# Gated cross-attention blocks on one Trainium2 core: GpSimd adds key blocks' exponentials, one TensorE product fewer in each sum, new order in the second half of a turn

## The chip, the cores and the metric

The kernel runs on one core of a Trainium2 chip. The metric is the device time in microseconds (us) of one execution. TensorE multiplies matrices, VectorE and ScalarE work element by element and read TensorE's results from PSUM, GpSimd works on SBUF, and SyncE (SP) issues the transfers.

## The reference

Two gated blocks, each an attention and a feed-forward part, over 8 batches of 256 rows and 512 features. The change touches only the second block's attention:

```python
q = rms_norm(linear(x, q_w, q_b), norm_q_w).reshape(B, L, NH, HD)      # 16 heads of 32
k_img = rms_norm(linear(ctx_img, k_img_w, k_img_b), norm_k_img_w)...   # 256 keys
v_img = linear(ctx_img, v_img_w, v_img_b)...
def attention(q, k, v):
    scores = jnp.einsum('bqhd,bkhd->bhqk', q, k) * scale
    probs = jax.nn.softmax(scores, axis=-1)
    return jnp.einsum('bhqk,bkhd->bqhd', probs, v)
x = x + tanh(g_xattn[1]) * (attention(q, k_img, v_img) @ o_w + o_b)    # then the quantised feed-forward part
```

## The kernel before, in words

The work has stages: a (first attention), b (first feed-forward part), and a last stage in which c (second attention) and d (second feed-forward part) of different batches are woven together, one batch (two tiles of 128 rows) at a time. Turns 3 to 7 of the last stage are alike. In turn n the engines work on four batches: f = n (queries and keys made), b = n - 1 (attention), c = n - 2 (attention's output, inputs of d), d = n - 3 (feed-forward part). Each engine has its program written out by hand, in a fixed order; engines meet at semaphores, and every instruction waits behind the ones ahead of it on its engine. PSUM has 8 banks: 0 to 3 take the score products, and `places.turn` writes for banks 4 to 7 the order in which results use them (w0 to w3 are weighings, ut the transposes of u, xt those of x, y output products).

For batch b and each group g of four heads, TensorE makes scores in `c_scores` (VectorE takes their maxima), and in the second half of the turn makes them again turned, keys on the partitions, in `c_probs`; ScalarE's `c_probs` (L1183) writes the exponentials to `PT`, 8 heads of 2 key blocks x 256 queries. TensorE's `c_weigh` (L786) multiplies them: 8 products with V (two key blocks, four heads), and 8 with a block of ones, which gives the softmax sums. Its products are fp32 and stand in the trace as two records each. VectorE's `c_weigh` (L1667, L1669) divides.

Around that, in the order of the second half:
- TensorE: `c_turn_q` transposes the queries of f after VectorE's `c_norm_q` (L1660); `d_turn_u` transposes u of d in two halves of 8 tiles after VectorE's `d_integers16` (L1762, two roundings from W to ARENA); `d_out_product` (L828) is the output product; `d_turn_q`; `c_turn_x` transposes x of f + 1 after `c_norm_x` (L1380). All transposes are L431.
- VectorE: `d_peak` and `d_inputs` of c (L1709 to L1730: small two-input and one-input operations, and four of 128x512), then the divisions, `stats` of f + 1 (L1370 to L1377), `d_integers16`, `d_store` (L1781), `c_norm_x`.
- GpSimd: `d_line`, roots of the norms (L2013, a power), `c_add_bias` (L2043, two in-place additions of 128x512 on X), `c_rstd` (L2013, for x of f + 1, waits for `stats`).
- SP loads K and V of later batches and stores finished rows; a V load waits for the last weighing of the batch that used the buffer.

Of the kernel before, what the change touches and what calls it, by code (L numbers as in the profile page):

```python
# [6 lines left out]
ALU = mybir.AluOpType  # L7
# [11 lines left out]
NB = 8  # L19
S = 256  # L20
TB = S // P
# [21 lines left out]
    a_kb a_ab a_sg a_gs a_s a_r a_abs a_kv a_kvr  # L43
    b_ve b_rstd b_xn b_xt b_xh b_xl b_g b_gu b_sg b_h b_sq b_acc b_fold b_ss b_me b_inv b_hh b_hl b_pr b_xy b_neg b_w1
    c_ve c_rstd c_xn c_xt c_xtr c_kss c_kinv c_kn c_kt c_ktr c_sc c_scr c_mhl c_mt c_mtr c_st c_ex
    c_pv c_pvr c_pjq c_qss c_qinv c_qn c_qt c_qtr c_po c_xo c_const c_vb c_vo c_vor c_bias c_xb
    d_st d_line d_hw d_xr d_tq d_q d_sv d_qt d_qtr d_g d_gu d_sg d_u d_so d_tu d_u16 d_ut d_utr d_utv d_y d_res
""".split())

# [103 lines left out]
def build(nc, x, ctx, ctxT, gates, w0, w1, wkv, wqo, vec, wnorm, cols, cst, masks, selq, selc, out):  # L153
    with ExitStack() as stack:
# [46 lines left out]
        kv_store = nc.dram_tensor("kv_store", (NB, 2, TB, P, D), F32, kind="Internal").ap()  # L201
        s = Sems(*[stack.enter_context(nc.semaphore("s_" + name)) for name in Sems._fields])

        late = 1
        by_bank = (2, 3, 0, 1)

# [55 lines left out]
        places.turn(1, ("pq0 kt0 w0 xt0", "pq1 tq1 w1 xt1", "mt tq0 w2", "kt1 w3"))  # L262
        places.turn(2, ("pq0 po0 w0", "po1 w1 qt1 xt1", "pq1 kt0 tq1 w2 xt0", "kt1 mt tq0 qt0 w3"))
        for turn in range(3, NB):
            places.turn(turn, ("g0 v1 g3 pq0 v6 v7 ut0.0 y0 xt0", "v0 po1 v3 g4 v5 g7 tq1 w1 w2 w3", "po0 g2 kt0 v4 pq1 w0 qt1 ut1.1 y1",
                               "g1 v2 kt1 g5 g6 mt tq0 ut0.1 qt0 ut1.0 xt1"))
        places.turn(NB, ("g0 v1 g3 v5 v7 w1 w3", "v0 po1 v3 g6 g7 ut0.0 y0", "po0 g2 g4 g5 mt w0 ut0.1", "g1 v2 v4 v6 w2"))
        places.last.update({n: (s.c_ex, 8 * NB) for n in range(4)})
        a, b, c = NB - 3, NB - 2, NB - 1
# [158 lines left out]
        def tensor_program(pe):  # L428
# [347 lines left out]
            def c_weigh(b, g):  # L776
                to, sem, value = bank_c(f"w{g}", b)
                pe.wait_ge(sem, value)
                pe.wait_ge((s.ld_v0, s.ld_v1)[b % 2], 16 * (b // 2 + 1))
                pe.wait_ge(s.c_ex, 8 * b + 2 * g + 2)  # L780
                for what in range(2):
                    for kb in range(TB):
                        for j in range(4):
                            h = 4 * g + j
                            lhs = keep["ones"] if what else bufW["V"][:, b % 2 * TB + kb, h * DH:(h + 1) * DH]
                            mm = pe.matmul(part(to, j)[:, what * S:(what + 1) * S], lhs, bufC["PT"][:, h % 8, kb * S:(kb + 1) * S],  # L786
                                           start=(kb == 0), stop=True, skip_group_check=True)
                mm.then_inc(s.c_pv, 1)
# [13 lines left out]
            def d_turn_u(d, t):  # L802
                for n in range(2):
                    to, sem, value = bank_c(f"ut{t}.{n}", d)
                    pe.wait_ge(sem, value)
                    pe.wait_ge(s.d_u16, 4 * d + 2 * t + n + 1)
                    turned(as16(to, BF16), [bufC["U16"][:, (8 * n + k) * P:(8 * n + k + 1) * P] for k in range(8)],
                           keep["identb"]).then_inc(s.d_ut, 1)
# [105 lines left out]
            for turn in range(3, NB):  # L914
                f, b, c, d = turn, turn - 1, turn - 2, turn - 3
                c_scores(b, 0)
                if turn == 3:
                    c_turn_x(3)
                d_value_gate(d, 0)
                c_project_out(c, 0)  # L920
                d_value_gate(d, 1)
                c_scores(b, 1)
                c_project_out(c, 1)
                d_value_gate(d, 2)
                d_value_gate(d, 3)
                c_scores(b, 2)
                c_turn_k(f)
                c_project_q(f, 0)
                d_value_gate(d, 4)
                d_value_gate(d, 5)  # L930
                c_scores(b, 3)
                c_project_q(f, 1)
                d_value_gate(d, 6)
                c_max_turn(b)
                d_value_gate(d, 7)
                c_probs(b, 0)
                c_turn_q(f)
                c_probs(b, 1)
                c_weigh(b, 0)
                d_turn_u(d, 0)  # L940
                c_probs(b, 2)
                c_weigh(b, 1)
                d_out_product(d, 0)
                d_turn_q(c)
                c_probs(b, 3)
                c_weigh(b, 2)
                d_turn_u(d, 1)
                if f + 1 < NB:
                    c_turn_x(f + 1)
                c_weigh(b, 3)  # L950
                d_out_product(d, 1)

            b, c, d = NB - 1, NB - 2, NB - 3
            c_scores(b, 0)
# [49 lines left out]
        def scalar_program(act):  # L1004
# [215 lines left out]
            def both(what, d, t):  # L1220
                what(d, t, 0)
                what(d, t, 1)
# [53 lines left out]
            for turn in range(3, NB):  # L1276
                f, b, c, d = turn, turn - 1, turn - 2, turn - 3
                d_gate(d, 0)
                d_gate(d, 1)
                c_square_k(f, 0)  # L1280
                c_square_k(f, 1)
                d_residual(d, 0)
                d_residual(d, 1)
                d_gate(d, 2)
                d_gate(d, 3)
                c_turn_k(f)
                c_square_q(f, 0)
                d_gate(d, 4)
                both(d_round_u, d, 0)
                d_gate(d, 5)  # L1290
                c_square_q(f, 1)
                d_gate(d, 6)
                d_gate(d, 7)
                warm(ACT.Exp)
                c_probs(b, 0)
                c_turn_q(f)
                c_probs(b, 1)
                both(d_turn_u, d, 0)
                c_probs(b, 2)
                both(d_round_u, d, 1)  # L1300
                d_turn_q(c)
                c_probs(b, 3)
                both(d_turn_u, d, 1)
                if f + 1 < NB:
                    c_turn_x(f + 1)
                warm(ACT.Silu)
# [47 lines left out]
        def vector_program(v):  # L1354
# [547 lines left out]
            for turn in range(3, NB):  # L1902
# [35 lines left out]
                if f + 1 < NB:  # L1938
                    c_norm_x(f + 1)
                c_weigh(b, 2)  # L1940
                c_weigh(b, 3)
                d_store(d, 1)

            b, c, d = NB - 1, NB - 2, NB - 3
            c_scores(b, 0)
# [65 lines left out]
        def pool_program(pool):  # L2011
# [67 lines left out]
            def c_queries_root(f, t):  # L2079
                pool.wait_ge(s.c_qss, 2 * f + t + 1)  # L2080
                pool.wait_ge(s.c_qn, max(0, 2 * (f - 1) + t + 1))
                root_of_mean(keep["sm"][:, 2, t:t + 1], keep["ss"][:, 2, t:t + 1], 1).then_inc(s.c_qinv, 1)

            own = Own(s.pool_own)
            for b in range(NB):
                if b == 0:
# [13 lines left out]
            for turn in range(1, NB + 2):  # L2100
                f, c = turn, turn - 2
                if f < NB:
                    c_keys_root(f)
                if turn == 1:
                    b_inverse(NB - 1)
                if c > 0:
                    d_line(c)
                if f < NB:
                    c_queries_root(f, 0)
                    c_queries_root(f, 1)  # L2110
                if c == 0:
                    d_line(c)
                if f < NB:
                    c_add_bias(f)
                if f + 1 < NB:
                    c_rstd(f + 1)

        with nc.Block() as block:
            block.sync(sync_program)
# [63 lines left out]
```

## Time and profile before

| what | value |
|---|---|
| median of 3 runs | 1129.12 us (1126.06 to 1130.04) |
| profiled execution, its own time | 1127.54 us |
| span of the profiled execution | 1125.5 us |
| TensorE busy in the span | 1092.2 us (97%) |
| VectorE, ScalarE, GpSimd busy | 839.0, 567.1, 117.9 us |
| turn 5's work on TensorE | 773.6 to 833.4 us |

The span runs from the first to the last instruction; the execution's own time has 2 us more around it. In the rows below, a line of the timeline is a run of like instructions: its start, how long it takes to the end of its last, the engine, the line of the kernel, the operation, its tiles, how many; in brackets the idle time of the engine before it and what ended it. Two fp32 passes of a product are two of the count. Consecutive groups on TensorE overlap by its pipeline, so the work of a group is the time from its start to the next group's start.

### The profile page before, as it was taken

Reading aid. Unit: us, or ns where it says so; the run is one execution under the profiler, and the core shown is the slowest. Engines: PE = TensorE matmul, PEld = TensorE weight load, DVE = VectorE, ACT = ScalarE, POOL = GpSimd, SP = SyncE. Lnnn points to the kernel's source line nnn. Section 1 sums busy time; section 2 is a strip of 40 time slices with the busy share of each in tenths; the row PEclk is TensorE's granted clock in tenths of the full one; section 3 lists DMA queues with packets and bytes.
Section 4 is the critical chain, followed back from the end, with each engine's and each line's share of the span. In section 5 each row is a group of like instructions: output and inputs, shape, how many; then the busy total and the mean of one; then the engine's idle time right before and its main releaser. Section 6 shows DMA issues by size and latency. Waiting matters only on the chain.

```text
span 1125.5 us, 25576 instructions
## 1 busy us (share of the span) xinstructions
PE 1092.2 (97%) x10386; PEld 662.7 (59%) x10386; DVE 839.0 (75%) x1437; ACT 567.1 (50%) x918; POOL 117.9 (10%) x212
## 2 busy tenths in 40 slices
PE   8899999999999999999999999899999999999998
PEld 3555555556777777777776655455554545454544
DVE  5788888778676657567566667887878788778786
ACT  4767666765433333333333353464554546372654
POOL 1101100110000000000001212020202030111010
PEclk9999999999999999999999999999999999999899
DMA  9565555433112011021010200101010101000001
GB/s 362 194 194 181 187 189 177 145 105 122 67 39 66 20 39 38 23 73 39 19 57 20 85 10 30 38 2 57 1 57 1 58 1 39 1 11 10 11 10 39
DMA packets 29267, 79.24 MB, mean 70 GB/s; under 512 B 3040, under 2 KB 3296, under 8 KB 28896
## 3 DMA queue, kind: packets, MB, share of 16 engines
q1 hardware_dynamic: 29152, 77.61, 21.0%
q8 instruction: 84, 1.38, 0.5%
q14 instruction: 31, 0.25, 0.1%
HBM read 65.02 MB, written 12.58 MB: 69 GB/s over the span
## 4 chain that ended last, share of the span: by engine, by line
PE 89%; DVE 4%; issue 3%; ACT 2%; POOL 1%; DMA 1%; SPq 0%; DVEq 0%; ACTq 0%; POOLq 0%
PE bank L693 10%; PE bank L589 10%; PE bank L590 10%; PE bank L675 10%; PE bank L551 9%; PE bank L798 8%; PE bank L431 5%; PE bank L828 5%; PE bank L786 5%; PE bank L748 3%; PE bank L767 2%; PE bank L456 2%; PE bank L516 2%; PE bank L483 2%; PE bank L504 2%
## 5 line engine op out<-in xcount | busy, mean ns | idle before, releaser
L589 PE MATMUL bank<-ARENA,W 128*128 128x256 f16 x1024 | 227.3, 273 | 0.7 <-issue 0.7
L590 PE MATMUL bank<-ARENA,W 128*128 128x256 f16 x1024 | 227.3, 273 | 0.0
L1006 ACT ACTIVATE ARENA<-bank 128x512 f32<-128x512 f32 (+3 forms) x143 | 92.9, 687 | 72.3 <-PE bank L431 35.5
L675 PE MATMUL bank<-W,ARENA 128*128 128x512 bf16 x512 | 120.8, 379 | 0.0
L551 PE MATMUL bank<-ARENA 128*128 128x512 f32 x256 | 117.7, 603 | 0.9 <-DMA ARENA<-in_wkv 0.9
L798 PE MATMUL bank<-W,ARENA 128*128 128x512 bf16 x512 | 117.7, 379 | 0.4 <-DVE W L1737 0.4
L693 PE MATMUL bank<-ARENA 128*128 128x512 f32 x256 | 116.9, 599 | 0.0
L589 PEld LDWEIGHTS bank<-ARENA,W 128*128 128x128 bf16 x1024 | 100.2, 98 | 19.1 <-issue 1.3
L590 PEld LDWEIGHTS bank<-ARENA,W 128*128 128x128 bf16 x1024 | 100.2, 98 | 18.0
L1006 ACT ACTIVATE ARENA<-ARENA 128x512 f16<-128x512 f32 x64 | 40.3, 630 | 133.3 <-DVE ARENA L1591 129.5
L1591 DVE SCALAR_TENSOR_TENSOR ARENA<-bank,ARENA 128x512 f32<-128x512 f32 x64 | 48.0, 750 | 72.3 <-PE bank L590 69.0
L2013 POOL TENSOR_TENSOR ARENA<-ARENA 128x2 f32<-128x2 f32 (+1 forms) x72 | 49.4, 686 | 491.1 <-DVE ARENA L1377 251.4
L1200 ACT ACTIVATE ARENA<-bank,ARENA 128x512 f32<-128x512 f32 x64 | 43.7, 685 | 104.6 <-PE bank L798 97.8
L798 PEld LDWEIGHTS bank<-W,ARENA 128*128 128x128 bf16 x512 | 48.8, 98 | 65.7 <-issue 12.5
L1121 ACT ACTIVATE ARENA<-bank 128x512 f32<-128x512 f32 x64 | 38.2, 596 | 91.1 <-PE bank L590 91.1
L1636 DVE TENSOR_REDUCE ARENA<-bank 128x4 f32<-128x1024 f32 x64 | 75.3, 1218 | 9.2 <-PE bank L748 9.2
L1597 DVE TENSOR_TENSOR ARENA<-ARENA 128x512 f16<-128x512 f32 x64 | 44.2, 691 | 47.3 <-ACT ARENA L1006 47.3
L551 PEld LDWEIGHTS bank<-ARENA 128*128 128x128 f32 x256 | 47.0, 191 | 55.2 <-issue 51.6
L675 PEld LDWEIGHTS bank<-W,ARENA 128*128 128x128 f16 x512 | 50.0, 99 | 48.8 <-issue 1.9
L1387 DVE TENSOR_REDUCE ARENA<-bank 128x4 f32<-128x512 f32 x64 | 58.2, 952 | 27.3 <-PE bank L456 27.3
L693 PEld LDWEIGHTS bank<-ARENA 128*128 128x128 f32 x256 | 46.6, 190 | 52.6 <-issue 51.6
L431 PE MATMUL bank<-ARENA 128*128 128x128 bf16 (+1 forms) x648 | 66.2, 249 | 11.2 <-DVE ARENA L1660 4.8
(181 smaller groups left out, 1799.6 us busy)
## 6 DMA issues: line engine op xcount, KB each, us to landing
W<-in_w SPq DMA_DIRECT2D x48, 512.0 KB, 4.3
ARENA<-in_w SPq DMA_DIRECT2D x24, 512.0 KB, 3.6
kv_store<-ARENA SPq DMA_DIRECT2D x32, 256.0 KB, 4.3
W<-kv_store SPq DMA_DIRECT2D x15, 512.0 KB, 4.1
ARENA<-in_ctxT SPq DMA_DIRECT2D x8, 512.0 KB, 3.9
X<-in_x SPq DMA_DIRECT2D x8, 512.0 KB, 5.7
ARENA<-in_ctx SPq DMA_DIRECT2D x8, 512.0 KB, 5.9
out<-X SPq DMA_DIRECT2D x16, 256.0 KB, 2.1
```

Source lines behind the costliest of these rows:

```text
L431: mm = pe.transpose(to[:, k * P:(k + 1) * P], tile, one)
L551: mm = pe.matmul(bank, bufA["KT"][:, b % 2 * KD + k, t * P:(t + 1) * P], W[:, k, :], start=(k == 0), stop=(k == KD - 1))
L589: pe.matmul(bank[:, i * S:(i + 1) * S], W0[:, at:at + P], xt_half(b, 0)[:, k, :], start=(k == 0), stop=False)
L590: mm = pe.matmul(bank[:, i * S:(i + 1) * S], W0[:, at:at + P], xt_half(b, 1)[:, k, :], start=False, stop=(k == KD - 1))
L675: mm = pe.matmul(banks[6 + t], hx(q, what)[:, i * S + t * P:i * S + (t + 1) * P], W0[:, UP_AT + m * D:UP_AT + (m + 1) * D], start=(m == 0 ...
L693: mm = pe.matmul(to, src[:, k, t * P:(t + 1) * P], WQ[w][:, k, :], start=(k == 0), stop=(w == "o" and k == KD - 1))
L786: mm = pe.matmul(part(to, j)[:, what * S:(what + 1) * S], lhs, bufC["PT"][:, h % 8, kb * S:(kb + 1) * S], start=(kb == 0), stop=True, skip ...
L798: mm = pe.matmul(to, QQ[d][:, t, k * P:(k + 1) * P], W1[:, at:at + D], start=(k == 0), stop=(k == KD - 1))
L828: mm = pe.matmul(to, UT[d, t][:, k * P:(k + 1) * P], W1[:, UP_AT + k * D:UP_AT + (k + 1) * D], start=(k == 0), stop=(k == KH - 1))
L1006: return act.activation(to, src, ACT.Copy)
L1387: got = v.tensor_reduce(NM[:, t, :, g % 2], bank[:, 0:4, t * P:t * P + (t + 1) * P], AX_X, ALU.max, negate=True)
L1636: got = v.tensor_reduce(NM[:, t, :, g], bank[:, 0:4, t * S:(t + 1) * S], AX_X, ALU.max, negate=True)
```

## The change

In turns 3 to 7 (batches 2 to 6, `paired`), GpSimd first subtracts the near value block from the far one in place (`c_values_apart`), and after each group's exponentials adds the far key block's exponentials to the near one's in place (`c_add_probs`, 128 partitions x 4 heads x 256). With P0 + P1 in the first place and V1 - V0 in the second, the two value products give P0 V0 + P1 V1 as before, and one product with ones gives the sum. TensorE's weighings each move one step later, `d_turn_q`, `d_turn_u` and `c_turn_x` come sooner; ScalarE and VectorE swap one pair each; the bias additions come before the second queries' root.

```diff
+        def paired(b):
+            return 2 <= b < NB - 1
...
-            places.turn(turn, ("g0 v1 g3 pq0 v6 v7 ut0.0 y0 xt0", "v0 po1 v3 g4 v5 g7 tq1 w1 w2 w3", "po0 g2 kt0 v4 pq1 w0 qt1 ut1.1 y1",
-                               "g1 v2 kt1 g5 g6 mt tq0 ut0.1 qt0 ut1.0 xt1"))
+            places.turn(turn, ("g0 v1 g3 pq0 v6 v7 ut0.0 y0 xt0", "v0 po1 v3 g4 v5 g7 tq1 w1 w2", "po0 g2 kt0 v4 pq1 w0 qt1 ut1.1 y1",
+                               "g1 v2 kt1 g5 g6 mt tq0 ut0.1 qt0 ut1.0 xt1 w3"))
...
             def c_weigh(b, g):
-                pe.wait_ge((s.ld_v0, s.ld_v1)[b % 2], 16 * (b // 2 + 1))
-                pe.wait_ge(s.c_ex, 8 * b + 2 * g + 2)
+                if paired(b):
+                    pe.wait_ge(s.c_dv, b - 1)
+                    pe.wait_ge(s.c_pa, 4 * (b - 2) + g + 1)
+                else:
+                    pe.wait_ge((s.ld_v0, s.ld_v1)[b % 2], 16 * (b // 2 + 1))
+                    pe.wait_ge(s.c_ex, 8 * b + 2 * g + 2)
                 for what in range(2):
-                    for kb in range(TB):
+                    for kb in range(1 if what and paired(b) else TB):
...
                 c_probs(b, 1)
+                d_turn_u(d, 0)
                 c_weigh(b, 0)
-                d_turn_u(d, 0)
                 c_probs(b, 2)
+                d_out_product(d, 0)
                 c_weigh(b, 1)
-                d_out_product(d, 0)
+                c_probs(b, 3)
                 d_turn_q(c)
-                c_probs(b, 3)
-                c_weigh(b, 2)
                 d_turn_u(d, 1)
                 if f + 1 < NB:
                     c_turn_x(f + 1)
+                c_weigh(b, 2)
+                d_out_product(d, 1)
                 c_weigh(b, 3)
-                d_out_product(d, 1)
...
+                c_probs(b, 3)
                 d_turn_q(c)
-                c_probs(b, 3)
...
                 c_weigh(b, 2)
+                d_store(d, 1)
                 c_weigh(b, 3)
-                d_store(d, 1)
...
+            def c_values_apart(b):
+                near, far = (bufW["V"][:, b % 2 * TB + kb, :] for kb in range(TB))
+                pool.wait_ge((s.ld_v0, s.ld_v1)[b % 2], 16 * (b // 2 + 1))
+                pool.tensor_tensor(far, far, near, ALU.subtract).then_inc(s.c_dv, 1)
+
+            def c_add_probs(b, g):
+                PT = bufC["PT"][:, g % 2 * 4:g % 2 * 4 + 4, :]
+                pool.wait_ge(s.c_ex, 8 * b + 2 * g + 2)
+                pool.tensor_tensor(PT[:, :, 0:S], PT[:, :, 0:S], PT[:, :, S:2 * S], ALU.add).then_inc(s.c_pa, 1)
...
                     c_queries_root(f, 0)
+                    if c > 0:
+                        c_add_bias(f)
                     c_queries_root(f, 1)
...
-                if f < NB:
+                if c <= 0:
                     c_add_bias(f)
+                if paired(f - 1):
+                    c_values_apart(f - 1)
+                    c_add_probs(f - 1, 0)
+                    c_add_probs(f - 1, 1)
                 if f + 1 < NB:
                     c_rstd(f + 1)
+                if paired(f - 1):
+                    c_add_probs(f - 1, 2)
+                    c_add_probs(f - 1, 3)
```

TensorE, from the first output product of a turn to the first scores of the next, before; L828 is the output product, L431 transposes, L767 and L771 `c_probs`, L786 the weighing (values, then ones), L748 the next turn's scores:

```order
L828 MATMUL bank<-W,ARENA 128x512 x16
L431 MATMUL bank<-ARENA 128x128 x8
L767 MATMUL bank<-W 128x256 x8
L771 MATMUL bank<-ARENA 128x256 x8
L786 MATMUL bank<-ARENA,W 32x256 x8
L786 MATMUL bank<-ARENA 32x256 x8
L431 MATMUL bank<-ARENA 128x128 x24
L786 MATMUL bank<-ARENA,W 32x256 x8
L786 MATMUL bank<-ARENA 32x256 x8
L828 MATMUL bank<-W,ARENA 128x512 x16
L748 MATMUL bank<-W 128x256 x8
```

The same stretch of TensorE in the change, where L835 is the output product, L434 transposes, L770 and L774 `c_probs`, L793 the weighing and L751 the scores:

```order
L835 MATMUL bank<-W,ARENA 128x512 x16
L793 MATMUL bank<-ARENA,W 32x256 x8
L793 MATMUL bank<-ARENA 32x256 x4
L770 MATMUL bank<-W 128x256 x8
L774 MATMUL bank<-ARENA 128x256 x8
L434 MATMUL bank<-ARENA 128x128 x32
L793 MATMUL bank<-ARENA,W 32x256 x8
L793 MATMUL bank<-ARENA 32x256 x4
L835 MATMUL bank<-W,ARENA 128x512 x16
L793 MATMUL bank<-ARENA,W 32x256 x8
L793 MATMUL bank<-ARENA 32x256 x4
L751 MATMUL bank<-W 128x256 x8
```

The second weighing has moved behind the first output product and the last two behind all transposes (32 in one block: 8 of `d_turn_q`, 16 of `d_turn_u`, 8 of `c_turn_x`); the products with ones are 4 instead of 8.

GpSimd, from the roots of the queries to the end of a turn, before (L2046 with L2013 is a root, L2043 a bias addition, the last row `c_rstd`):

```order
L2046 TENSOR_SCALAR ARENA<-ARENA 128x1 [waits s_c_qn,s_c_qss]
L2013 TENSOR_TENSOR ARENA<-ARENA 128x1 [waits s_pool_own]
L2046 TENSOR_SCALAR ARENA<-ARENA 128x1 [waits s_c_qn,s_c_qss]
L2013 TENSOR_TENSOR ARENA<-ARENA 128x1 [waits s_pool_own]
L2043 TENSOR_TENSOR X<-X,ARENA 128x512 [waits s_c_xn,s_c_bias]
L2043 TENSOR_TENSOR X<-X,ARENA 128x512
L2013 TENSOR_TENSOR ARENA<-ARENA 128x2 [waits s_c_ve]
```

The same of GpSimd in the change (L2053 with L2020 a root, L2050 a bias addition, L2094 the subtraction of the values, L2099 the additions of exponentials, and L2020 of 128x2 `c_rstd`):

```order
L2053 TENSOR_SCALAR ARENA<-ARENA 128x1 [waits s_c_qn,s_c_qss]
L2020 TENSOR_TENSOR ARENA<-ARENA 128x1 [waits s_pool_own]
L2050 TENSOR_TENSOR X<-X,ARENA 128x512 [waits s_c_xn,s_c_bias]
L2050 TENSOR_TENSOR X<-X,ARENA 128x512
L2053 TENSOR_SCALAR ARENA<-ARENA 128x1 [waits s_c_qn,s_c_qss]
L2020 TENSOR_TENSOR ARENA<-ARENA 128x1 [waits s_pool_own]
L2094 TENSOR_TENSOR W<-W 128x512 [waits s_ld_v1]
L2099 TENSOR_TENSOR ARENA<-ARENA 128x4x256 [waits s_c_ex] x2
L2020 TENSOR_TENSOR ARENA<-ARENA 128x2 [waits s_c_ve]
L2099 TENSOR_TENSOR ARENA<-ARENA 128x4x256 [waits s_c_ex] x2
```

The two bias additions have moved between the two roots, and five operations are new, two of them behind `c_rstd`.

## Rows read from the trace of the kernel before

**Rows 1.** The page: engine, busy us, share of the span, instructions; then the chain.

```profile
PE 1092.2 (97%) x10386; PEld 662.7 (59%) x10386; DVE 839.0 (75%) x1437; ACT 567.1 (50%) x918; POOL 117.9 (10%) x212
...
PE 89%; DVE 4%; issue 3%; ACT 2%; POOL 1%; DMA 1%; SPq 0%; DVEq 0%; ACTq 0%; POOLq 0%
```

**Rows 2.** Busy time by engine in turn 5's stretch, granted clock, DMA share, GB/s.

```profile
773.60:833.40 59.80, 58.64 (x485) 30.62 (x484) 48.63 (x81) 32.68 (x48) 9.24 (x20) 1.00 0.08 26
```

**Rows 3.** Timeline of TensorE, second half of turn 5.

```profile
809.91 1.06 PE L431 MATMUL bank<-ARENA 128*128 128x128 f32 x8 [0.88 <-DVE ARENA L1660]
...
812.41 1.07 PE L786 MATMUL bank<-ARENA,W 128*32 128x256 f32 x16
813.30 1.05 PE L786 MATMUL bank<-ARENA 128*32 128x256 f32 x16
814.28 1.07 PE L431 MATMUL bank<-ARENA 128*128 128x128 bf16 x16
...
818.44 3.63 PE L828 MATMUL bank<-W,ARENA 128*128 128x512 bf16 x16
821.90 0.61 PE L431 MATMUL bank<-ARENA 128*128 128x128 bf16 x8
822.44 1.15 PE L767 MATMUL bank<-W 32*128 32x256 f32 x16
...
823.74 1.07 PE L786 MATMUL bank<-ARENA,W 128*32 128x256 f32 x16
...
825.60 1.51 PE L431 MATMUL bank<-ARENA 128*128 128x128 bf16 x20
827.40 0.66 PE L431 MATMUL bank<-ARENA 128*128 128x128 f32 x4 [0.28 <-ACT ARENA L1006]
...
833.43 1.15 PE L748 MATMUL bank<-W 32*128 32x256 f32 x16
```

**Rows 4.** Timeline of ScalarE, the same stretch: exponentials of groups 0, 1, 3.

```profile
809.14 1.94 ACT L1183 ACTIVATE ARENA<-bank 128x1024 f32<-128x1024 f32 x2
...
812.52 1.94 ACT L1183 ACTIVATE ARENA<-bank 128x1024 f32<-128x1024 f32 x2
...
823.92 1.94 ACT L1183 ACTIVATE ARENA<-bank 128x1024 f32<-128x1024 f32 x2 [0.45 <-PE bank L771]
```

**Rows 5.** Timeline of VectorE, the same stretch.

```profile
816.84 1.75 DVE L1667 RECIPROCAL ARENA<-bank 128x256 f32<-128x256 f32 x1
...
818.97 1.27 DVE L1370 BATCH_NORM_STATS2 ARENA<-X 128x6 f32<-128x512 f32 x2
...
820.67 1.76 DVE L1667 RECIPROCAL ARENA<-bank 128x256 f32<-128x256 f32 x1
...
822.80 1.28 DVE L1762 TENSOR_SCALAR ARENA<-W 128x1024 bf16<-128x1024 f32 x2
...
824.66 1.00 DVE L1380 TENSOR_SCALAR ARENA<-X,ARENA 128x512 f32<-128x512 f32 x2
```

**Rows 6.** Timelines of 806.90 to 807.60: GpSimd's second bias addition and VectorE's roundings.

```profile
806.68 0.74 DVE L1762 TENSOR_SCALAR ARENA<-W 128x1024 bf16<-128x1024 f32 x1
...
806.83 1.72 POOL L2043 TENSOR_TENSOR X<-X,ARENA 128x512 f32<-128x512 f32 x1
...
807.35 1.76 DVE L1762 TENSOR_SCALAR ARENA<-W 128x1024 bf16<-128x1024 f32 x1
```

**Rows 7.** All instructions of L2043, of L1716: shortest, median, longest in ns.

```profile
L2043 POOL TENSOR_TENSOR X<-X,ARENA x16: 1267/1272/1724, 620.7 to 986.4; 128x512 f32<-128x512 f32 x16
...
L1716 DVE TENSOR_TENSOR ARENA<-ARENA x8: 152/160/657, 702.6 to 1077.8; 128x2 f32<-128x2 f32 x8
```

**Rows 8.** Timeline of GpSimd: `c_rstd` in turn 5.

```profile
820.81 0.71 POOL L2013 TENSOR_TENSOR ARENA<-ARENA 128x2 f32<-128x2 f32 x1 [12.26 <-DVE ARENA L1377]
```

**Rows 9.** After turn 7: TensorE's timeline at a wait, then all engines' busy time behind it.

```profile
1042.45 2.47 PE L767 MATMUL bank<-W 32*128 32x256 f32 x14 [1.28 <-ACT ARENA L1183]
...
1043.00:1049.80 6.80, 6.73 (x58) 3.41 (x60) 2.23 (x6) 4.23 (x5) 0.00 (x0) 0.50 0.01 2
```

More of the change, by code:

```diff
@@ L45 @@
     c_ve c_rstd c_xn c_xt c_xtr c_kss c_kinv c_kn c_kt c_ktr c_sc c_scr c_mhl c_mt c_mtr c_st c_ex
-    c_pv c_pvr c_pjq c_qss c_qinv c_qn c_qt c_qtr c_po c_xo c_const c_vb c_vo c_vor c_bias c_xb
+    c_dv c_pa c_pv c_pvr c_pjq c_qss c_qinv c_qn c_qt c_qtr c_po c_xo c_const c_vb c_vo c_vor c_bias c_xb
     d_st d_line d_hw d_xr d_tq d_q d_sv d_qt d_qtr d_g d_gu d_sg d_u d_so d_tu d_u16 d_ut d_utr d_utv d_y d_res
```

## The prediction

> **What bounds the kernel now.** I read the page first: TensorE is busy for 97% of the span and the chain that ended last lies on it for 89% [rows 1]. The reader should see that anything taken off TensorE counts in full, and anything that makes it wait costs in full. Then one turn of the last stage as a stretch: of 59.80 us TensorE works 58.64 at full clock [rows 2], so at most 1.2 us of idling is there to be won. Then TensorE's timeline through the second half of that turn (turn 5; the others to turn 6 repeat it): two holes only, 0.88 us before the first transposes of the queries and 0.28 us before those of x [rows 3]. Last, what ScalarE and VectorE do under it [rows 4, 5] and how GpSimd and VectorE behave where they meet [rows 6, 7].
>
> **What is removed.** A weighing now runs 812.41 to 814.28: 0.89 us of value products, then 0.98 us of sums from 813.30 [rows 3]. The change drops the second key block of the sums: 4 of 16 products, half of the sums' 0.89 us of work (the 0.89 of the equal first half), 0.44 us. A weighing then takes 1.43 us. `paired` is true for batches 2 to 6, that is in turns 3 to 7, with 5 x 4 weighings: 20 x 0.44 = 8.8 us off TensorE, 1.76 us a turn.
>
> **Bias sooner.** GpSimd's two bias adds fall from 805.6 to 808.6 now; VectorE's first two roundings to u16 meet them and take 0.74 and 1.76 us where a pair alone takes 1.28 [rows 5, 6]. Moved ahead of the second root, the adds lie near 797 to 800 us, ahead of these roundings. In their old place stands one subtraction of 1.27 us [rows 7], over by 806.9. So VectorE's L1660, for which TensorE waits 0.88 us [rows 3], comes about 0.85 us sooner. I count that as nothing: behind the transposes stands the second score product, which needs the exponentials that ScalarE makes from 809.14 to 811.08 [rows 4]; it ends near 812.4 as before. The hole moves and is not closed.
>
> **What GpSimd's additions cost.** No such addition is in the trace. The nearest row is an in-place addition of 512 columns: 1.27 us alone [rows 7]. Twice that, 2.54 us, bounds 1024 columns from above. From below: GpSimd's fixed part can't exceed the 0.71 us of its small power [rows 8], giving 2.54 - 0.71 = 1.83. I take 2.35, near the top, since GpSimd's cost should mostly go with columns. All reading and writing is in SBUF, as in that row.
>
> **Where they meet VectorE.** [Rows 6] show it one by one: the second bias add, issued at 806.83, ends at 808.55, and the rounding issued at 807.35 ends only at 809.11. Each waits for the other's whole instruction, in order of issue. The two-element addition of two SBUF inputs shows the same once, 0.657 us against 0.160 [rows 7]. Reductions and operations fed from PSUM show no such stretch. The longest hold seen is some 1.2 us, but each wait there ends with the other's end and not before, so I let a new addition hold VectorE for its whole 2.35 us; if a hold ended at the 1.2 us seen, the milder case B would come out. The Trainium skill (SBUF — State Buffer, Who interferes with whom) says of this that one of the two is blocked for the other's whole instruction, however long that is. By that rule the sum is the main one below, +24.9 us; by holds of 1.2 us it would be near B's +7.3. The trace agrees with the rule as far as its 1.2 us go.
>
> **The new second half, in rows' durations.** Everything on the clock of [rows 3 to 5]; signals take 0.1 us.
> 1. TensorE ends the second score product at 812.4, transposes u (1.0) to 813.4. The first addition starts when the exponentials end, 811.1, ends 813.5. Weighing 0: 813.6 to 815.0, a wait of 0.2.
> 2. Score product 2 (1.30, as 822.44 to 823.74) to 816.3; the output product (3.46, as 818.44 to 821.90) to 819.8; weighing 1 to 821.2; score product 3 to 822.5; transposes of q (0.54) to 823.1. TensorE finds no wait in these.
> 3. VectorE: the second addition starts with the end of the second exponentials, 814.46 [rows 4], and holds until 816.9. Before weighing 0, VectorE has d_inputs to finish, two-input and rounding work which ends at 816.84 now [rows 5]. Stopped by additions 1 and 2, it ends at 818.5. Weighing 0's division (2.13, as 816.84 to 818.97) to 820.6, stats (1.70) to 822.3, weighing 1's division (2.13) to 824.4.
> 4. GpSimd's root for the next x waits for those stats and takes 0.7 [rows 8], to 823.1; only then addition 3, to 825.45. Exponentials 3 end 1.48 + 1.94 us after score product 3 begins, as in [rows 3, 4]: 824.6. So addition 4 is queued directly behind addition 3.
> 5. VectorE's two roundings to u16, half t = 1, want to start at 824.4. The first is held to 825.45 and ends at 826.0; addition 4 goes next, to 828.2; the second rounding ends at 828.75. Then d_store and c_norm_x (0.66 + 1.0, [rows 5]) to 830.4.
> 6. TensorE wants those roundings at 823.1: it waits 3.0 us for the first, transposes 0.45, waits 2.3 for the second, 0.45, waits 0.6 and 0.1 for the two halves of xn. It goes on at 831.0: weighing 2 to 832.4, output product to 835.9, weighing 3 to 837.3.
>
> Now the turn ends at 833.43 [rows 3]: 3.9 us a turn more, in the four turns 3 to 6. Turn 7 normalises no further x, so there is no root and no c_norm_x: addition 3 is done before the roundings begin at 823.4, and the turn comes out 0.3 us shorter. Sum: 4 x 3.9 - 0.3 = 15.3 us. VectorE's last division and d_store swap places; in the next turn a score product and a value and gate product stand before the first product that needs the division (2.1 us), so that is free. SP's V load waits for the last weighing and its stores for d_store, as now; a V block is read two turns after its load is issued, so that costs nothing, nor does the subtraction's wait for it. GpSimd's next task after addition 4 (828.2) is the keys' root of the next turn, which waits for that turn's squares anyway. Weighing 3's move to the fourth bank list makes it wait for xt1's reader, which is done before it.
>
> **The clock.** After turn 7 the trace shows TensorE idling 1.28 us before 1042.45 and then granted 0.50 of its clock, 1.2 GHz, for 6.80 us [rows 9], almost wholly filled with work: 3.4 us lost. The new turn idles about 6 us out of 8. I expect such a fall in each of the four turns, but part of it, some 2 us, inside the stall: (6.8 - 2) / 2 = 2.4 us each, bounds 0 and 3.4. 4 x 2.4 = 9.6 us.
>
> Total 15.3 + 9.6 = 24.9 us on the profiled execution's 1127.54: 1152.4. The median of the runs is 1129.12, 1.6 above, so I say 1153.
>
> **Rivals.**
> - A without the clock's fall, or with it in some turns: 1143 to 1149. For it: the turn's hole of 0.88 us leaves the clock at 1.00 [rows 2, 3].
> - B, holds shorter or d_inputs not caught: stats end near 820, addition 3 ends at 823.75, the roundings pass at 823.4 to 824.9, but addition 4 still holds c_norm_x until 827.3. The turn is 1.9 us longer: 4 x 1.9 - 0.3 = +7.3, 1135 to 1136; with the clock's fall (up to 4 x 3.4) up to 1149.
> - C, no contention that matters: even so, the roundings stand behind weighing 1's division (821.3 + 2.1), and TensorE, arriving at 823.1, waits 1.1 + 0.15 + 0.6 + 0.2 us for them, xn and a bank. That eats the 1.76 + 0.28 won: the turn ends at 833.6, in all about 0: 1128 to 1130.
> - Faster, the other side: the waits at u16 and xn don't arise. It decides by whether VectorE has divided weighing 1 and rounded u16 by 823.1, which needs it 1.1 us or more ahead of case C. Then 8.8 + 4 x 0.28 = 9.9 us is kept, and if the 0.88 us holes close too, 5 x 0.88 more: 1119 to 1115. Against it: VectorE runs without a break through [rows 5].
> - Worse than A: one-element operations of d_scale_u are held too, and additions take 2.54: 4.8 us a turn, clock 3.4: 1127.5 + 4 x 8.2 = 1160.
>
> **How the numbers follow.** A with the clock 0.45, A without 0.15, B 0.15, C 0.10, faster 0.09, worse 0.06. A measurement of this kernel tells about 0.5% (5.6 us) from no change. Slower by more: A, B, worse and a little of C, 0.82; within: 0.10; faster: 0.08. The range goes from B's lower part, 1133, to the worse case, 1160; what lies under it is C and faster (0.19). A's own range is 1143 to 1157.
>
> **What would show it.** In the trace after: sum products halved; the four additions at 2.35 us or longer each; VectorE's u16 roundings of the second half at 1.5 us and more instead of half of 1.28; TensorE's idle time before the bf16 transposes released by that rounding, several us a turn, in turns 3 to 6 and not 7; a granted clock below 1.00 right after. I am wrong if GpSimd's additions take under 1.9 us, if VectorE's d_inputs pass unharmed, or if the clock stays full through the stall.

## The result: slower, 1149.5 us against 1129.2

The changed kernel took 1149.52 us (median of 4 runs, 1146.46 to 1151.32), the kernel before 1129.21; the ratio is 1.0182, 95% interval 1.0165 to 1.0199. The profiled execution took 1151.32 us with a span of 1149.3. I had said 1153, range 1133 to 1160, and slower with 0.82.

The page of the changed kernel, lines as in [rows 1]:

```profile
PE 1098.7 (96%) x10226; PEld 665.8 (58%) x10226; DVE 856.0 (74%) x1437; ACT 568.0 (49%) x918; POOL 173.3 (15%) x237
...
PE 83%; DVE 9%; issue 4%; ACT 2%; DMA 2%; POOL 1%; DVEq 0%; SPq 0%; ACTq 0%; POOLq 0%
```

TensorE has fewer instructions and is busy longer: part of them ran at half clock. VectorE's share of the chain went up from 4% to 9%.

Busy time by engine, granted clock, DMA share and GB/s in the stretch of [rows 2], of the changed kernel, and below it that of turn 7. (The stretch of [rows 2] is turn 4. I called it turn 5; turns 4, 5 and 6 are alike, so no number hangs on it.)

```profile
784.10:849.20 65.10, 59.94 (x459) 31.16 (x456) 52.87 (x81) 32.90 (x48) 20.46 (x25) 0.95 0.08 25
...
979.00:1039.80 60.80, 58.20 (x448) 29.61 (x444) 47.38 (x74) 31.59 (x46) 19.44 (x24) 0.97 0.07 23
```

From first scores to first scores, turns 4, 5, 6 and 7 take 65.07, 64.96, 64.91 and 60.80 us, each 59.86 before. Turn 3 from its last scores on takes 39.86 instead of 34.43. Together +21.7 us.

One thing in the description of the change has to be put right, since an argument below rests on it: `d_turn_q`, the transposes of q, does not come sooner. Before, it stood ahead of the last `c_probs`; in the change it stands behind it, on TensorE and on ScalarE. Only `d_turn_u` and `c_turn_x` come sooner.

Timeline of TensorE in the second half of turn 4, changed kernel; it answers to [rows 3], 10.5 us later on the clock:

```profile
820.85 1.74 PE L770 MATMUL bank<-W 32*128 32x256 f32 x14 [0.26 <-ACT ARENA L1190]
...
824.20 1.07 PE L793 MATMUL bank<-ARENA,W 128*32 128x256 f32 x16 [0.18 <-POOL ARENA L2099]
825.06 0.64 PE L793 MATMUL bank<-ARENA 128*32 128x256 f32 x8
...
833.21 0.62 PE L434 MATMUL bank<-ARENA 128*128 128x128 bf16 x8
836.37 0.79 PE L434 MATMUL bank<-ARENA 128*128 128x128 bf16 x8 [2.54 <-ACT ARENA L1013]
839.12 3.05 PE L434 MATMUL bank<-ARENA 128*128 128x128 bf16 x16 [1.96 <-DVE ARENA L1769]
842.10 1.73 PE L793 MATMUL bank<-ARENA,W 128*32 128x256 f32 x16
...
849.18 1.15 PE L751 MATMUL bank<-W 32*128 32x256 f32 x16
```

The sums are 8 records instead of 16 (the row of 825.06). The two large holes, 2.54 and 1.96 us, stand before the two halves of u's transposes. The first is named after ScalarE and not after VectorE; experiments 1 and 7 say what there is to that.

Timelines of GpSimd and VectorE under it, narrow windows; they answer to [rows 5, 6]:

```profile
833.33 2.34 POOL L2099 TENSOR_TENSOR ARENA<-ARENA 128x1024 f32<-128x1024 f32 x1
...
834.65 1.57 DVE L1769 TENSOR_SCALAR ARENA<-W 128x1024 bf16<-128x1024 f32 x1
...
835.64 2.79 POOL L2099 TENSOR_TENSOR ARENA<-ARENA 128x1024 f32<-128x1024 f32 x1
...
836.15 2.83 DVE L1769 TENSOR_SCALAR ARENA<-W 128x1024 bf16<-128x1024 f32 x1
```

Read by order of issue: addition 3 (833.33) runs to 835.67; rounding 1 (834.65) waits for that and ends at 836.22; addition 4 (835.64) waits for that and ends at 838.43; rounding 2 (836.15) waits for that and ends at 838.98. The two roundings took 1.28 us together before. Earlier in the turn the same happens to VectorE's d_inputs. The two-element addition meets the first addition of exponentials (821.69 to 824.05), the first 128x512 operation meets the second (825.07 to 827.43); alone they take 0.16 and 0.48 us:

```profile
823.63 0.44 DVE L1723 TENSOR_TENSOR ARENA<-ARENA 128x2 f32<-128x2 f32 x1
...
825.12 2.59 DVE L1733 TENSOR_SCALAR ARENA<-ARENA 128x512 f32<-128x512 f32 x1
```

And the clock, the changed kernel's stretches at half clock in turns 4 and 7:

```profile
836.70:843.50 6.80, 4.74 (x37) 3.24 (x38) 3.84 (x4) 3.92 (x5) 1.73 (x1) 0.50 0.00 1
1031.20:1034.60 3.40, 3.40 (x37) 1.87 (x34) 0.00 (x0) 3.01 (x4) 1.51 (x1) 0.50 0.20 77
```

TensorE worked 4.74 us of the first, which costs 2.4 us at half clock; it worked all 3.40 us of the second, which costs 1.7.

### The profile page after: what moved, and what is told of

It is laid out like the page before. It is cut to its first block, busy times and chain, and to the rows that moved or that the text cites. A ratio compares the mean times of both kernels' runs of the same rounds, so it can differ in the third digit from the quotient of the medians.

```text
span 1149.3 us, 25281 instructions
## 1 busy us (share of the span) xinstructions
PE 1098.7 (96%) x10226; PEld 665.8 (58%) x10226; DVE 856.0 (74%) x1437; ACT 568.0 (49%) x918; POOL 173.3 (15%) x237
## 3 DMA queue, kind: packets, MB, share of 16 engines
q8 instruction: 82, 1.34, 0.5%
## 4 chain that ended last, share of the span: by engine, by line
PE 83%; DVE 9%; issue 4%; ACT 2%; DMA 2%; POOL 1%; DVEq 0%; SPq 0%; ACTq 0%; POOLq 0%
PE bank L696 10%; PE bank L592 10%; PE bank L593 10%; PE bank L678 9%; PE bank L554 9%; PE bank L805 8%; PE bank L434 5%; PE bank L835 4%; PE bank L793 3%; PE bank L751 3%; PE bank L519 2%; PE bank L486 2%; PE bank L459 2%; PE bank L507 2%; DVE ARENA L1769 1%
## 5 line engine op out<-in xcount | busy, mean ns | idle before, releaser
L2020 POOL TENSOR_TENSOR ARENA<-ARENA 128x2 f32<-128x2 f32 (+1 forms) x72 | 49.6, 688 | 463.4 <-DVE ARENA L1620 236.4
L434 PE MATMUL bank<-ARENA 128*128 128x128 bf16 (+1 forms) x648 | 74.3, 266 | 25.6 <-ACT ARENA L1013 12.2
L434 PEld LDWEIGHTS bank<-ARENA 128*128 128x128 bf16 (+1 forms) x648 | 60.2, 128 | 41.4 <-issue 23.6
L1674 DVE RECIPROCAL ARENA<-bank 128x256 f32<-128x256 f32 x32 | 56.1, 1755 | 34.4 <-PE bank L793 34.3
L554 PEld LDWEIGHTS bank<-ARENA 128*128 128x128 f32 x256 | 47.5, 193 | 55.9 <-issue 53.1
```

Of the source, the lines that this page charges most:

```text
L434: mm = pe.transpose(to[:, k * P:(k + 1) * P], tile, one)
L554: mm = pe.matmul(bank, bufA["KT"][:, b % 2 * KD + k, t * P:(t + 1) * P], W[:, k, :], start=(k == 0), stop=(k == KD - 1))
L1674: v.reciprocal(bufC["rec"], to[:, S:2 * S]).then_inc(*own.up())
L2020: return pool.tensor_tensor(to, src, keep["minus_half"][:, 0:n], ALU.pow)
```

## Experiments

Theory L: GpSimd's additions hold VectorE's operations on SBUF (the held operation does nothing until the other has ended), and TensorE waits for those. Theory Q, formed from the holes of 2.54 and, in turn 7, 2.04 us named after ScalarE: bank 7 takes `qt0` and then `ut1.0`; in the new order ScalarE copies `qt0` out behind the last exponentials, and TensorE's transposes of u wait for that copy. Rivals: the order alone costs, or the additions alone. Turn lengths are from the profiles, TensorE's first scores to first scores. Each ratio is to the kernel before as timed next to that run (medians 1127.89 to 1129.32 us).

**1. No additions.** The weighing waits for the exponentials; nothing adds the key blocks, so half of each sum and part of each value product is missing.

```diff
-                    pe.wait_ge(s.c_pa, 4 * (b - 2) + g + 1)
+                    pe.wait_ge(s.c_ex, 8 * b + 2 * g + 2)
...
-                    c_add_probs(f - 1, 0)    (and 1, 2, 3)
```

> The change without GpSimd's four additions a turn (the subtraction of the values stays; the weighing waits for the exponentials; the sums take the near key block alone, so part of the softmax sum and of the output is left out). Theory L, the additions hold VectorE's two u16 roundings: TensorE's wait of 1.96 us for the rounding (turn 4 of the changed kernel) disappears, turns 4 to 6 fall from 65.0 to about 60 us, and the roundings pair takes 1.3 instead of 4.3 us. Theory Q, the wait of 2.5 us named after ScalarE is for PSUM bank 7, whose reader (the copy of the transposed q) stands behind the last exponentials on ScalarE: about 2 us of it stays here too, as in turn 7 of the changed kernel (2.04). With both the time comes to 1127 to 1133 us, by how often the clock still falls. If the holds were not what costs, turns 4 to 6 would stay near 65 us.

1132.64 us, ratio 1.0034 (1.0019 to 1.0050). Turns 4 to 6: 60.33, 61.41, 61.41 (the longer two each with 3.4 us at half clock). TensorE's timeline in turn 4:

```profile
828.69 1.55 PE L434 MATMUL bank<-ARENA 128*128 128x128 bf16 x20 [2.04 <-ACT ARENA L1013]
830.49 0.66 PE L434 MATMUL bank<-ARENA 128*128 128x128 f32 x4 [0.24 <-ACT ARENA L1013]
```

The wait for VectorE is gone, the 2.04 us after ScalarE stay: both theories hold their ground. The median is 16.9 us below the change's, of the 20.3 by which the change is slower: so much hangs on the additions being there.

**2. Order alone.** `paired(b)` returns False: full sums, no operation of GpSimd added.

> The new sequence of all engines and the bias sooner, but no pairing: full sums, no additions, no subtraction. Theory Q: the order alone costs. The two old holes of a turn (0.88 and 0.28 us) go, new ones of about 0.3, 2.0 and 0.5 us come before the second transposes of u and those of x; turns 4 to 6 take 61 to 63 us instead of 59.86, with falls of the clock where they come, in all 1134 to 1146 us. Rival: the order is neutral by itself and only the additions cost: 1127 to 1131 us.

1139.41 us, ratio 1.0097 (1.0077 to 1.0117): the order isn't neutral. Turns 4 and 5 take 62.05 us, turn 6 63.38 (with a fall of the clock), turn 7 60.71; the same wait of 2.04 us stands before u's transposes. Without additions to cover, the order costs some 11 us.

**3. Bias sooner alone.**

```diff
                     c_queries_root(f, 0)
+                    if c > 0:
+                        c_add_bias(f)
                     c_queries_root(f, 1)
...
-                if f < NB:
+                if c <= 0:
                     c_add_bias(f)
```

> The kernel before with only the bias additions moved ahead of the second queries' root. My prediction counted this at nothing: VectorE's roundings pass in 1.3 us instead of 2.4, L1660 ends 1.1 us sooner, TensorE's hole of 0.88 us before the queries' transposes goes, but 0.3 to 0.9 us of waiting for the exponentials comes in its place: 0 to -3 us in all, 1126 to 1130. Rival: the hole closes for good, 5 x 0.88 = -4.4 us: 1124 to 1125.

1128.72 us, ratio 1.0006 (0.9994 to 1.0018). All turns take 59.86 us as before. TensorE's timeline in turn 4:

```profile
809.15 1.09 PE L431 MATMUL bank<-ARENA 128*128 128x128 f32 x8
810.50 1.74 PE L767 MATMUL bank<-W 32*128 32x256 f32 x14 [0.26 <-ACT ARENA L1183]
```

The transposes have no hole ahead of them now, and the score product behind them has: 0.26 us, and 0.6 us inside it (1.74 instead of 1.15). VectorE's gain of 0.9 us ends at ScalarE's exponentials.

**4. What the sums are worth.** The kernel before, with half of each sum in turns 3 to 7 left out.

```diff
-                    for kb in range(TB):
+                    for kb in range(1 if what and 2 <= b < NB - 1 else TB):
```

> The kernel before with only the products of the second key block with ones left out in turns 3 to 7 (so those softmax sums lack half of their terms); nothing else is moved. It prices what the change takes off TensorE: 20 x 0.44 = -8.8 us if every product on TensorE counts, 1119 to 1122. Rival: ScalarE's exponentials or VectorE's divisions set the pace of the second half, so that half of it or more turns into waits: 1124 to 1128.

1123.04 us, ratio 0.9958 (0.9944 to 0.9972): -4.9 us, between the two. Turns 4 to 6 fall to 59.25 to 59.27, by 0.6 us and not 1.76; turn 7 falls by 1.7. Over the five turns that is 4.1 us of 8.8. TensorE's timeline in turn 4:

```profile
829.18 1.07 PE L786 MATMUL bank<-ARENA,W 128*32 128x256 f32 x16 [1.01 <-DVE ARENA L1669]
```

The last weighing waits for VectorE's division of the one before, which holds its bank: in the old order a third of the saving can be had in each of turns 3 to 6 and less than half in all, even if GpSimd's additions were free. Both halves of my expectation met in the middle.

**5. The fourth addition late.** It waits until VectorE has rounded u and normalised x.

```diff
                 pool.wait_ge(s.c_ex, 8 * b + 2 * g + 2)
+                if g == 3:
+                    pool.wait_ge(s.d_u16, 4 * (b - 2) + 4)
+                    if b + 2 < NB:
+                        pool.wait_ge(s.c_xn, 2 * (b + 2) + 2)
```

> The changed kernel, but GpSimd's fourth addition of a turn also waits until VectorE has rounded the second half of u and normalised the next x. Nothing else is moved, and TensorE needs that addition only after an output product. Theory L: the second rounding and c_norm_x are no longer held; TensorE's 1.76 to 1.96 us wait for the rounding goes, the roundings take at most 1.6 + 0.7 us instead of 1.58 + 2.83, and turns 4 to 6 fall from 65.0 to between 62 and 63.5 us (the 2.0 to 2.5 us wait for bank 7 stays, and a fall of the clock may). In all 1138 to 1144 us. If the wait were set by something else, the turn would stay near 65 us or grow, since the addition comes later.

1138.99 us, ratio 1.0090 (1.0075 to 1.0105). Turns 62.29, 61.92, 61.42. Timelines of VectorE, TensorE and GpSimd in turn 4:

```profile
830.92 2.18 DVE L1769 TENSOR_SCALAR ARENA<-W 128x1024 bf16<-128x1024 f32 x2
...
832.64 3.66 PE L434 MATMUL bank<-ARENA 128*128 128x128 bf16 x24 [2.55 <-ACT ARENA L1013]
...
834.84 2.35 POOL L2103 TENSOR_TENSOR ARENA<-ARENA 128x1024 f32<-128x1024 f32 x1 [2.89 <-DVE ARENA L1387]
```

An operation that begins 3 us later in its turn (54.5 us after its start instead of 51.5) makes the kernel 10.5 us faster: the roundings pass in 2.18 instead of 4.32 us and TensorE's second hole is gone. The clock gains as well: behind the first hole, still 2.55 us, it stays at half for 3.4 us in turn 4 and not for 6.8. This is the direct proof of L. The time is inside what I expected; two of the turns are shorter than my 62 to 63.5 us.

**6. Additions cut in four.** Each in four operations of 128x256.

```diff
-                pool.tensor_tensor(PT[:, :, 0:S], PT[:, :, 0:S], PT[:, :, S:2 * S], ALU.add).then_inc(s.c_pa, 1)
+                for j in range(4):
+                    got = pool.tensor_tensor(PT[:, j, 0:S], PT[:, j, 0:S], PT[:, j, S:2 * S], ALU.add)
+                got.then_inc(s.c_pa, 1)
```

> The changed kernel with each addition of 128x1024 cut into four of 128x256. Theory L, each operation holds the other engine for its own whole length and they take turns: four short ones hold VectorE's rounding for at most 0.7 us each; the second rounding falls from 2.83 to at most 1.4 us, but the four additions take about 2.9 us instead of 2.36 and c_norm_x is held twice. Turns 4 to 6: 62.5 to 64.5 us, in all 1140 to 1147. Rival: the engines share by bandwidth and not by instruction: then cutting changes nothing for VectorE (roundings together 4.3 us) and costs GpSimd's fixed times, 65 us or more a turn.

1139.33 us, ratio 1.0104 (1.0079 to 1.0128). Turns 62.46, 62.12, 63.25. Timelines of GpSimd and VectorE in turn 4:

```profile
828.03 6.83 POOL L2100 TENSOR_TENSOR ARENA<-ARENA 128x256 f32<-128x256 f32 x8
...
829.35 1.82 DVE L1769 TENSOR_SCALAR ARENA<-W 128x1024 bf16<-128x1024 f32 x2
```

More work on GpSimd, 6.83 us for two additions, and less waiting on VectorE: 1.82 us for the pair of roundings instead of 4.32. Part of that comes back at the normalisation of x, which takes 1.84 us instead of 0.98. The time and turn 5 are a little below the 1140 us and 62.5 us that I had as lower ends. The rival of shared bandwidth, the roundings still at 4.3 us together, is out: the hold goes by instruction. The Trainium skill (SBUF — State Buffer, Who interferes with whom) says that the loser is blocked for the other's whole instruction; with roundings of 1.57 and 2.83 us beside long additions and 1.82 us for the pair beside short ones, these runs agree.

**7. Transposes of q early,** on TensorE and ScalarE, as in the kernel before.

```diff
-                c_probs(b, 3)
                 d_turn_q(c)
+                c_probs(b, 3)
```

> The changed kernel with the transposes of q and ScalarE's copy of them ahead of the last scores' product and exponentials, as in the kernel before. Theory Q: bank 7 is free before TensorE asks for it. In turn 7, without held roundings, TensorE's wait of 2.04 us falls to about 1.0 (then it is the roundings behind the division) and the turn from 60.8 to 59.3 to 60.2 us. In turns 4 to 6 the held rounding ends within 0.1 us of the copy, so the wait only changes its name from ScalarE to VectorE and the turn stays at 64.5 to 65.2 us. In all 1145 to 1150. Rival: bank 7 is what costs, turns 4 to 6 fall by 2 us or more, 1140.

1149.70 us, ratio 1.0187 (1.0172 to 1.0202). Turns 4 to 6 stay (65.24, 65.05, 64.95); the hole of 2.54 us is there, now named after VectorE's L1769. Turn 7 falls from 60.80 to 58.65, more than I expected (59.3 to 60.2). TensorE's timeline in turns 4 and 7:

```profile
832.71 0.61 PE L434 MATMUL bank<-ARENA 128*128 128x128 bf16 x8 [2.54 <-DVE ARENA L1769]
...
1026.60 1.21 PE L434 MATMUL bank<-ARENA 128*128 128x128 bf16 x16 [1.18 <-DVE ARENA L1769]
```

So the name in the changed kernel's row misled: of ScalarE's two copies only the first frees the bank that TensorE asks for. The timeline of ScalarE in turn 4 of the changed kernel has both in one row:

```profile
835.22 1.09 ACT L1013 ACTIVATE ARENA<-bank 128x512 bf16<-128x512 bf16 x2
```

The second ends at 836.31, just after the rounding (836.22), and so gets the blame; the first ended about half way. In turns 3 to 6 the held rounding is what TensorE waits for and the bank lies hidden under it; taking the bank's wait away gives nothing there.

**8. Pairing in the old order.** The additions, with all three engines' order and the banks of the kernel before.

> The pairing (subtraction, four additions, half of the sums' products) and the bias sooner, but with the order of TensorE, ScalarE and VectorE and the banks of the kernel before. If the new order is there to cover GpSimd's additions, this is worse: weighing 0 waits 1.2 us for its addition, weighing 1 about 0.8, weighing 2 about 2.3 (its addition stands behind the root that waits for the stats), and the roundings are held: turns 4 to 6 take 62.5 to 65 us, in all 1140 to 1152. Rival: the order is what costs and pairing is harmless: 1122 to 1130.

1149.02 us, ratio 1.0161 (1.0118 to 1.0204); turns 64.64, 64.64, 63.01. TensorE's timeline in turn 4, before the first and the third weighing:

```profile
820.00 1.07 PE L793 MATMUL bank<-ARENA,W 128*32 128x256 f32 x16 [1.17 <-POOL ARENA L2099]
...
831.64 1.07 PE L793 MATMUL bank<-ARENA,W 128*32 128x256 f32 x16 [1.11 <-POOL ARENA L2099]
```

In turn 7 the hole before the third weighing is 2.19 us. The second, for which I had 0.8, has none. In the change all that is left of these holes is 0.18. The new order does cover the additions, but by itself it costs 11 us (experiment 2), and the roundings are held in either: in time the two orders with additions come out alike, 1149.0 and 1149.5 us.

**9 to 11. Taking the costs away one by one.** Experiment 5 with one wait more: the second addition stands back until VectorE has finished d_inputs (9). Then the early transposes of q as well (10). Then VectorE rounds the second half of u before it divides weighing 1 (11).

```diff
+                if g == 1:
+                    pool.wait_ge(s.d_q, 2 * (b - 1) + 2)
...
-                c_weigh(b, 1)
                 d_integers16(d, 1)
+                c_weigh(b, 1)
```

> The changed kernel with two of GpSimd's additions made to wait: the second until VectorE has finished d_inputs, the fourth until it has rounded u and normalised x. No work is left out. Theory L: d_inputs is held by 1.6 us less, so stats, root and third addition come 1.6 us sooner, the first rounding passes in 0.7 us, and the second too. What stays is the wait for bank 7 (about 2.0 us) and then some 0.3 us for x. Turns 4 to 6: 60.3 to 61.5 us against 61.4 with the fourth addition alone late and 65.0 in the change; in all 1131 to 1137 us. Against L: no gain over the fourth addition alone, 1139.

> As the one with two additions made to wait, and the transposes of q with their copy ahead of the last exponentials, so that bank 7 is free sooner. Both theories together: every cost that I name is gone, TensorE waits about 1.1 us for the rounding that stands behind weighing 1's division and about 1 us for x. Turns 4 to 6: 59.7 to 60.7 us, in all 1127 to 1133, no different from the kernel before within 0.5%. If something else cost in the change, several us a turn would be left.

> As the one before it (two additions late, q early), and VectorE rounds the second half of u before it divides weighing 1. TensorE then finds u rounded when it comes to its transposes and waits only 0.8 to 1.3 us for x. Turns 4 to 6: 58.9 to 59.8 us against 59.86 in the kernel before, in all 1121 to 1128 us. If the division of weighing 1, now later, holds bank 5 and x up, it stays at 60 us a turn or more, 1129 or above.

| | median us | ratio (interval) | turns 4, 5, 6 | turn 7 |
|---|---|---|---|---|
| the change | 1149.52 | 1.0182 (1.0165 to 1.0199) | 65.07, 64.96, 64.91 | 60.80 |
| 9 | 1134.47 | 1.0036 (1.0021 to 1.0052) | 60.57, 61.63, 60.57 | 60.84 |
| 10 | 1129.28 | 1.0006 (0.9990 to 1.0021) | 60.06, 60.06, 60.07 | 58.65 |
| 11 | 1124.59 | 0.9957 (0.9944 to 0.9969) | 59.75, 59.76, 59.75 | 58.65 |

All three times fell where they were expected. The turns are those of the profiled execution. In 9 that was one of the two quickest of eight (1129.68 us; the others lie between 1133.79 and 1137.07, most at a lower mean clock), so its turns are shorter than those of the median run; turn 5, with its fall of the clock, is already above the 61.5 us that I expected at most. TensorE's timeline in turn 4 of experiment 10, at the transposes of u and of x:

```profile
824.93 1.21 PE L434 MATMUL bank<-ARENA 128*128 128x128 bf16 x16 [1.18 <-DVE ARENA L1769]
826.65 1.08 PE L434 MATMUL bank<-ARENA 128*128 128x128 f32 x8 [0.51 <-DVE ARENA L1387]
```

and of experiment 11, at the two transposes of x:

```profile
825.61 0.63 PE L434 MATMUL bank<-ARENA 128*128 128x128 f32 x4 [0.70 <-DVE ARENA L1387]
826.93 0.66 PE L434 MATMUL bank<-ARENA 128*128 128x128 f32 x4 [0.70 <-ACT ARENA L1013]
```

With the holds and the bank out of the way what is left in 10 is VectorE's own queue, and in 11 1.4 us for x. Version 11 beats both kernels, by 4.7 us against the one before. Its turns account for 0.1 us each in 3 to 6 and 1.2 in 7, 1.6 in all; the rest is that the stretch after turn 7 took 109.5 us in its profile, without a fall of the clock, and 112.5 in the profile before, with one. What decides whether that stretch keeps its clock stays open; the same code has it both ways.

**12. Turn 7 alone** paired and in the new order (q early, the second addition late), the rest as before with the bias sooner.

> The kernel before, with pairing and the new order in turn 7 alone (there no x is normalised), with the transposes of q early and the second addition behind d_inputs; the bias is sooner in all turns. Turn 7 falls from 59.86 to between 58 and 58.9 us, the others stay: -1 to -2 us, 1126 to 1128, which a measurement can hardly tell from no change. Rival: turn 7 is held as well, no gain.

1128.15 us, ratio 0.9997 (0.9986 to 1.0008). Turn 7 takes 58.66 us, the others 59.86 as before: the 1.2 us are there in the profile and too small for the runs, whose median is just above the 1128 us that I had as upper end.

## Why the prediction was right, and where it was off

- **Sums, 1.76 us a turn off TensorE:** right as work: the sums' records are halved, 0.55 us from start to next start instead of 0.98.
- **Bias, counted at nothing:** right, and shown by experiment 3: the hole of 0.88 us moves behind the transposes.
- **Additions, taken at 2.35 us:** the changed kernel's 20 additions have a median of 2.360 and a shortest of 2.342 us. The weighing waits 0.18 us for the first of them, as the 0.2 of step 1.
- **Holds in order of issue:** right one by one. Step 5 has the roundings begin at 824.4, end at 826.0 and 828.75; moved by the 10.5 us of turn 4's later start that is 834.9, 836.5 and 839.3. Measured: 834.65, 836.2 and 839.0. Experiments 5, 6 and 9 show it as the cause.
- **Holes, 3.9 us a turn:** in turn 4 TensorE waited 2.54 and 1.96 where I had 3.0, 2.3 and then 0.7 for x. The wait for x didn't show, since TensorE, at half clock, took 3 us for what I had at 1.5. A turn came out 5.1 to 5.2 us longer (turn 3: 5.4), against 3.9 + 2.4 = 6.3 predicted.
- **Clock, 2.4 us a turn:** 2.4 us in turn 4's row above, by a stretch of 6.8 us in which TensorE worked 4.74. Right, with the 2 us that I had put inside the stall, and it fell in all of turns 3 to 6.
- **Missed: bank 7.** Step 6 let TensorE wait for VectorE's rounding alone. `ut1.0` takes the bank of `qt0`, which ScalarE copies out behind the last exponentials, 2.0 us after TensorE asks for it in every turn with the new order (experiments 1 and 2, where the hole ends with that copy). In turns 3 to 6 of the change it hid under the held rounding (experiment 7). In turn 7, where no rounding is held, it is what I got wrong: +0.94 us and not -0.3. Added are 2.04 us of waiting, 1.7 us of half clock and 1.0 us of small holes (0.26 and 0.6 at the second score product, 0.18 at the first weighing); saved are 1.76 us of sums and two old holes, 0.88 and 1.34 us (the second in the row of 1007.59 below). It also means that my case C, about 0 without contention, was a little too mild: experiment 1 has 60.33 us a turn even where the clock stays up. With the bank's wait gone too, experiment 10 has 60.06, which is C's sum (833.6 instead of 833.43).
- **The sum:** turns 3 to 7 give +21.7 us against 24.9. The profiled execution is 23.8 us longer than the one before it: 5.1 us more before turn 3's last scores, and 3.0 us less after turn 7, where the clock fell before and not after. Of the 5.1 us, 3.7 are there when the second attention's first scores begin (640.3 against 636.6 us; 636.0 in experiment 7, whose order is the same up to there), and 1.5 come from a fall of the clock at 717 us that the profile before does not have. So 2.1 of the 23.8 us lie outside the turns that the change touches, and that 23.8 is so near to 24.9 is in part luck. The holes were priced too high in turns 3 to 6 and too low in turn 7.

Turn 7 in TensorE's timelines: the second old hole, before, and the wait for bank 7, in the change:

```profile
1007.59 1.07 PE L786 MATMUL bank<-ARENA,W 128*32 128x256 f32 x16 [1.34 <-DVE ARENA L1669]
...
1030.82 1.56 PE L434 MATMUL bank<-ARENA 128*128 128x128 bf16 x16 [2.04 <-ACT ARENA L1013]
```

So the forecast stood on the right step. What would have made it wrong is to price the saving alone: experiment 4 shows that in the old order even free additions bring less than half of it.

## What to carry to other kernels

Before moving work to GpSimd, look at VectorE's operations in the same stretch, and at who waits for them. Held here were the roundings and scalings from SBUF to SBUF (128x1024 and 128x512) and the addition of two SBUF inputs; reductions, operations fed from PSUM and one-element operations were not. A long operation on GpSimd holds each of the first kind until it ends, and two queued ones catch two in a row. The cure is cheap: let the GpSimd operation wait until VectorE's are through (10.5 us here for one addition of each turn), if its own reader comes late enough. When an order is changed to cover a new latency, walk through every bank's list as well as the data: the new wait was for a bank whose reader had been moved back on a third engine.

## What the runs showed that I had not expected

- Holding is not a matter of GpSimd's total: 6.83 us of short additions cost less than 5.09 us of long ones (experiment 6 against the change, 1139.3 and 1149.5 us).
- VectorE's one-element operations ran at their usual 0.15 to 0.27 us beside an addition, the two-element addition of two SBUF inputs was held (a median of 0.441 us, 0.160 before). I had kept both possibilities open.
- A fall of TensorE's clock costs as much as the hole before it. In turn 4 of the change the half clock begins at 836.6 us, 0.3 us after the hole of 2.54 us has ended and before the second hole, and lasts 6.8 us (2.4 us lost). In experiment 9 a single hole of 2.04 us left the clock alone in turns 4 and 6 (60.57 us) and not in turn 5 (61.63). A hole of 2.35 us, before 713.76 in the kernel before and before 717.45 in the change, left it at 1.00 in the one profile and was followed by 3.4 us at half clock in the other. Why it falls after one hole and not after another of the same length stays open.
